# Graph layer in FP32 pieces: the first two column groups interleaved, the first half of adjacency rounded on VectorE, seven x tiles loaded later

## What is computed

```python
h   = maximum(layernorm(x), 0)          # mean and variance over the 256 features, eps 1e-5
agg = adj @ h
out = x + relu(agg @ W.T + b)
```

## Time and profile before

| what | us |
| --- | --- |
| median of 3 runs (380.69 to 380.96) | 380.95 |
| the profiled execution | 380.8 |
| span of its profile | 379.0 |
| TensorE busy in it | 375.1 |
| VectorE, ScalarE, GpSimd busy | 212.2, 181.8, 50.1 |

### The profile page before, as it was taken

How to read it: one execution, slowest core, us unless ns; L and a number is a source line. 1 busy time by engine, 2 the same in 40 slices (tenths; PEclk the granted TensorE clock), 3 DMA queues, 4 the chain that set the end, 5 groups by cost and what they waited for, 6 DMA issues and landing times.

```text
span 379.0 us, 4516 instructions
## 1 busy us (share of the span) xinstructions
PE 375.1 (99%) x1651; PEld 308.1 (81%) x1651; DVE 212.2 (56%) x294; ACT 181.8 (48%) x228; POOL 50.1 (13%) x88
## 2 busy tenths in 40 slices
PE   8999999999999999999999999999999999999997
PEld 4888888888888888888888888888888888888885
DVE  5999988874744453535564544444464444444424
ACT  5888776764443434343643343433355243434341
POOL 5687732320010000000001000000000100000000
PEclk9999999999999999999999999999999999999999
DMA  7989877577659565655566856565656775555203
GB/s 263 369 301 304 275 256 258 185 235 256 210 186 317 174 215 178 208 177 209 176 206 207 294 178 209 178 205 184 201 189 195 256 242 195 187 202 185 92 2 111
DMA packets 22774, 80.25 MB, mean 212 GB/s; under 512 B 2496, under 2 KB 2880, under 8 KB 22752
## 3 DMA queue, kind: packets, MB, share of 16 engines
q1 hardware_dynamic: 19584, 68.30, 54.1%
q0 software_dynamic: 3168, 11.67, 8.6%
HBM read 75.76 MB, written 4.19 MB: 211 GB/s over the span
## 4 chain that ended last, share of the span: by engine, by line
PE 98%; DMA 1%; DVE 0%; ACT 0%; POOL 0%; issue 0%; POOLq 0%
PE bank L421 92%; PE bank L463 6%; DMA x_sb<-x_dram 1%; ACT adj_hi L346 0%; POOL rstd L204 0%; ACT h_sb L352 0%; DVE out_sb L320 0%; DVE stats L240 0%; DVE mean_var L245 0%; DVE var_eps L249 0%; POOLq L200 0%
## 5 line engine op out<-in xcount | busy, mean ns | idle before, releaser
L421 PE MATMUL bank<-adj_hi,h_sb 128*128 128x512 f32 x1024 | 254.3, 389 | 0.2 <-ACT adj_hi L346 0.2
L229 DVE TENSOR_TENSOR adj_lo<-adj_in,adj_hi 128x1024 fp32r<-128x1024 f32 x126 | 154.6, 1227 | 145.7 <-ACT adj_hi L342 145.5
L421 PEld LDWEIGHTS bank<-adj_hi,h_sb 128*128 128x128 f32 x1024 | 192.0, 188 | 40.5 <-issue 0.5
L342 ACT ACTIVATE adj_hi<-adj_in 128x1024 fp32r<-128x1024 f32 x126 | 133.5, 1060 | 176.7 <-PE bank L421 174.5
L421 PE MATMUL bank<-adj_lo,h_sb 128*128 128x512 f32 x512 | 137.5, 389 | 0.0
L421 PEld LDWEIGHTS bank<-adj_lo,h_sb 128*128 128x128 f32 x512 | 96.1, 188 | 20.0
L204 POOL TENSOR_TENSOR rstd<-var_eps,minus_half 128x1 f32<-128x1 f32 x32 | 30.5, 954 | 3.4 <-DVE var_eps L249 0.8
L221 POOL DMA_DIRECT2D out_t_dram<-out_sb x3 | 2.2, 726 | 211.0 <-DVE out_sb L320 211.0
L352 ACT ACTIVATE h_sb<-centred,rstd 128x256 fp32r<-128x256 f32 x32 | 16.0, 499 | 3.6 <-POOL rstd L204 3.2
L362 ACT ACTIVATE centred<-x_sb,neg_mean 128x256 f32<-128x256 f32 x31 | 15.5, 500 | 2.1 <-DVE neg_mean L264 1.9
L270 DVE SCALAR_TENSOR_TENSOR h_sb<-centred,rstd,h_sb 128x256 fp32r<-128x256 f32 x32 | 15.3, 477 | 1.0 <-ACT h_sb L352 1.0
(11 more groups left out here) (25 smaller groups left out, 42.7 us busy)
## 6 DMA issues: line engine op xcount, KB each, us to landing
adj_in<-adj_t_dram SPq DMA_DIRECT2D x126, 512.0 KB, 3.6
xt_sb<-x_t_dram POOLq DMA_DIRECT2D x4, 1024.0 KB, 7.4
x_sb<-x_dram POOLq DMA_DIRECT2D x7, 512.0 KB, 6.5
out_t_dram<-out_sb POOLq DMA_DIRECT2D x3, 1024.0 KB, 4.9
adj_in<-adj_t_dram SPq DMA_DIRECT2D x4, 256.0 KB, 4.8
out_t_dram<-out_sb SPq DMA_DIRECT2D x3, 256.0 KB, 2.0
x_sb<-x_dram POOLq DMA_DIRECT2D x3, 128.0 KB, 4.6
w_sb<-w_t_dram POOLq DMA_DIRECT2D x1, 256.0 KB, 6.0
```

Source lines behind the costliest of these rows:

```text
L229: nc.vector.tensor_tensor(adj_lo[:, k, :], adj_in[:, k, :], adj_hi[:, k, :].bitcast(fp32), ALU.subtract).then_inc(s_lo, 1)
L342: nc.scalar.activation(adj_hi[:, k, :], adj_in[:, k, :], ACT.Copy).then_inc(s_hi, 1)
L421: last = nc.tensor.matmul(bank(g, kb, c)[:], h_sb[:, t, hp, kb * P:(kb + 1) * P], adj_parts[ap][:, n % U, chunk(c)], start=(t == 0 and (hp ...
```

## The change

- The order of units is now a list, `UNITS`. Groups 0 and 1 alternate tile by tile for tiles 0 to 23 (`LAG` = 8), then group 0 finishes with tiles 24 to 31, then group 1; groups 2 and 3 follow as before. The places of the split and of the output are counted from each group's end (`end_of`, `SPLIT`, `OUT`), so that for group 0 they are at units 60 and 64, for group 1 at 68 and 72. TensorE's wait for the products with w_lo moves to the first split.
- The halves that are loaded first are now both of tile 0: units 0 and 1 are groups 0 and 1 of it.
- `first_rounded`: VectorE makes `adj_hi` of the first half, between `centre_first` and `h_rest(0)`. ScalarE waits for that before it rounds the second half.
- SP issues x tile 1 after the third half of adjacency. GpSimd issues tiles 2 and 3 after `root(0)`, tiles 4 to 7 after `root(1)`.
- Both engines' lists around the first units are reordered: the layer norm of tile n - 1 is now finished beside unit n.
- The matmuls on constants become 9 of 512 columns and 1 of 256.

```diff
-    WARM_UP = 10
-    WARM_ON = 3
+    WARM_UP = 9
+    WARM_ON = 1
+    LAG = 8
+    UNITS = [(g, t) for t in range(TILES - LAG) for g in range(2)]
+    UNITS += [(g, t) for g in range(2) for t in range(TILES - LAG, TILES)]
+    UNITS += [(g, t) for g in range(2, GROUPS) for t in range(TILES)]
+        def end_of(g):
+            return max(n for n, u in enumerate(UNITS) if u[0] == g) + 1
+        SPLIT = {end_of(g) + SPLIT_AT: g for g in range(LAST)}
+        OUT = {end_of(g) + OUT_AT: g for g in range(LAST)}
...
             load_chunk(1, 0)
+            load_x(sp, 1)
             load_chunk(1, 1)
...
-            for i in range(1, U):
-                load_x(pool, i)
...
                 root(t)
                 if t == 0:
+                    load_x(pool, 2)
+                    load_x(pool, 3)
+                if t == 1:
                     load_x(pool, U)
...
+            def first_rounded():
+                dve.wait_ge(s_early[0][0], 16)
+                nc.vector.tensor_copy(adj_hi[:, 0, chunk(0)], adj_in[:, 0, chunk(0)]).then_inc(s_hi, 1)
...
             centre_first()
+            first_rounded()
             h_rest(0)
+            early_rest(0, 0)
+            early_rest(0, 1)
+            early_rest(1, 0)
             moments(1)
             minus_mean(1)
...
+            for n in range(EARLY, TILES + 1):
+                if n < TILES:
+                    moments(n)
+                    minus_mean(n)
+                adj_rest(n)
+                h_rest(n - 1)
...
             h_rounded(0)
-            early_rounded(0, 0)
+            act.wait_ge(s_hi, 1)
             early_rounded(0, 1)
+            early_rounded(1, 0)
+            early_rounded(1, 1)
             centre(1)
...
+            for n in range(EARLY, TILES + 1):
+                if n > EARLY:
+                    centre(n - 1)
+                adj_rounded(n)
+                h_rounded(n - 1)
...
+            def early_unit(n):
+                pe.wait_ge(s_hhi, 1)
+                pe.wait_ge(s_hi, made_chunk(n, 0))
+                add_up(n, [0], 0, 0)
+                pe.wait_ge(s_hlo, 1)
+                add_up(n, [0], 1, 0)
+                pe.wait_ge(s_hi, made_chunk(n, 1))
+                add_up(n, [1], 0, 0)
+                pe.wait_ge(s_lo, made_chunk(n, 0))
+                add_up(n, [0], 0, 1)
+                add_up(n, [1], 1, 0)
+                pe.wait_ge(s_lo, made_chunk(n, 1))
+                add_up(n, [1], 0, 1).then_inc(s_pe, 1)
```

More of the change, by code:

```diff
@@ L128, in x_piece, with made_chunk, made_unit @@
             return next(i for i, (a, b) in enumerate(X_PIECES) if a <= t < b)
-        def made_chunk(t, c):
-            return CHUNKS * t + c + 1
-        def made_tile(n):
+        def end_of(g):
+            return max(n for n, u in enumerate(UNITS) if u[0] == g) + 1
+        SPLIT = {end_of(g) + SPLIT_AT: g for g in range(LAST)}
+        OUT = {end_of(g) + OUT_AT: g for g in range(LAST)}
+        def made_chunk(n, c):
+            return CHUNKS * n + c + 1
+        def made_unit(n):
             return made_chunk(n, CHUNKS - 1) if n < EARLY else CHUNKS * EARLY + n - EARLY + 1
@@ L157, in _, with load_chunk @@
         def _(sp):
-            def load_chunk(t, c):
-                sp.dma_start(adj_in[:, t, chunk(c)], adj_v[:, t, chunk(c)]).then_inc(s_early[t][c], 16)
+            def load_chunk(n, c):
+                g, t = UNITS[n]
+                at = g * GW + c * BANK
+                sp.dma_start(adj_in[:, n, chunk(c)], adj_v[:, t, at:at + BANK]).then_inc(s_early[n][c], 16)
             def load_adj(n):
-                g, t = divmod(n, TILES)
+                g, t = UNITS[n]
                 if n >= U:
-                    sp.wait_ge(s_hi, made_tile(n - U))
-                    sp.wait_ge(s_lo, made_tile(n - U))
+                    sp.wait_ge(s_hi, made_unit(n - U))
+                    sp.wait_ge(s_lo, made_unit(n - U))
                 sp.dma_start(adj_in[:, n % U, :], adj_v[:, t, g * GW:(g + 1) * GW]).then_inc(s_adj[n % U], 16)
@@ L172, in _ @@
             load_chunk(1, 0)
+            load_x(sp, 1)
             load_chunk(1, 1)
-            for n in range(EARLY, GROUPS * TILES):
+            for n in range(EARLY, len(UNITS)):
                 load_adj(n)
@@ L227, in adj_rest, with early_rest @@
                 k = n % U
-                dve.wait_ge(s_hi, made_tile(n))
+                dve.wait_ge(s_hi, made_unit(n))
                 nc.vector.tensor_tensor(adj_lo[:, k, :], adj_in[:, k, :], adj_hi[:, k, :].bitcast(fp32),
                                         ALU.subtract).then_inc(s_lo, 1)
[L232 to L235, removed]
+            def first_rounded():
+                dve.wait_ge(s_early[0][0], 16)
+                nc.vector.tensor_copy(adj_hi[:, 0, chunk(0)], adj_in[:, 0, chunk(0)]).then_inc(s_hi, 1)
+            def early_rest(n, c):
+                dve.wait_ge(s_hi, made_chunk(n, c))
+                nc.vector.tensor_tensor(adj_lo[:, n, chunk(c)], adj_in[:, n, chunk(c)],
+                                        adj_hi[:, n, chunk(c)].bitcast(fp32), ALU.subtract).then_inc(s_lo, 1)
             def moments(t):
@@ L277, in _ @@
             centre_first()
+            first_rounded()
             h_rest(0)
+            early_rest(0, 0)
+            early_rest(0, 1)
+            early_rest(1, 0)
             moments(1)
             minus_mean(1)
[L281 to L286, removed]
-            early_rest(1, 1)
[L288 to L297, removed]
+            early_rest(1, 1)
+            for n in range(EARLY, TILES + 1):
[4 more added lines that the diff above has]
+                h_rest(n - 1)
             dve.wait_ge(s_b, 16)
@@ L322, in make_out @@
                                                    op0=ALU.max, op1=ALU.add).then_inc(s_sum, 1)
[L324 to L330, removed]
+            for n in range(TILES + 1, len(UNITS)):
+                if n in SPLIT:
+                    sums_rest(SPLIT[n])
+                if n in OUT:
+                    make_out(OUT[n])
+                adj_rest(n)
             sums_rest(LAST)
@@ L342, in adj_rounded, with early_rounded @@
                 nc.scalar.activation(adj_hi[:, k, :], adj_in[:, k, :], ACT.Copy).then_inc(s_hi, 1)
-            def early_rounded(t, c):
-                act.wait_ge(s_early[t][c], 16)
-                nc.scalar.activation(adj_hi[:, t, chunk(c)], adj_in[:, t, chunk(c)], ACT.Copy).then_inc(s_hi, 1)
+            def early_rounded(n, c):
+                act.wait_ge(s_early[n][c], 16)
+                nc.scalar.activation(adj_hi[:, n, chunk(c)], adj_in[:, n, chunk(c)], ACT.Copy).then_inc(s_hi, 1)
             def h_rounded(t):
@@ L385, in sums_rounded @@
                 if g < LAST:
-                    act.wait_ge(s_pe, (g + 1) * TILES)
+                    act.wait_ge(s_pe, end_of(g))
                 for i, (c, kb) in enumerate(GROUP_BANKS):
@@ L400, in _ @@
             act.wait_ge(s_b, 16)
[L401 to L407, removed]
+            for n in range(TILES + 1, len(UNITS)):
+                if n in SPLIT:
+                    sums_rounded(SPLIT[n])
+                if n in OUT:
+                    add_bias(OUT[n])
+                adj_rounded(n)
             add_bias(LAST)
@@ L415, in _, with add_up @@
             adj_parts = (adj_hi, adj_lo)
-            def add_up(g, t, chunks, hp, ap):
-                n = g * TILES + t
+            def add_up(n, chunks, hp, ap):
+                g, t = UNITS[n]
                 for kb in range(KB):
@@ L425, in add_up, with sum_unit @@
                 return last
[L427 to L442, removed]
+            def early_unit(n):
[11 more added lines that the diff above has]
+                add_up(n, [1], 0, 1).then_inc(s_pe, 1)
+            def sum_unit(n, chunks, arrived):
+                g, t = UNITS[n]
                 for hp, ap in PASSES:
@@ L446, in sum_tile @@
                             if g == 0:
-                                pe.wait_ge(s_hhi, n + 1)
-                            pe.wait_ge(s_hi, made_tile(n))
+                                pe.wait_ge(s_hhi, t + 1)
+                            pe.wait_ge(s_hi, made_unit(n))
                         elif ap == 1:
-                            pe.wait_ge(s_lo, made_tile(n))
+                            pe.wait_ge(s_lo, made_unit(n))
                         elif g == 0:
-                            pe.wait_ge(s_hlo, n + 1)
-                    last = add_up(g, t, chunks, hp, ap)
+                            pe.wait_ge(s_hlo, t + 1)
+                    last = add_up(n, chunks, hp, ap)
                 return last
@@ L482, in _ @@
             warm_up(WARM_ON, BANK // 2)
[L483 to L489, removed]
+            for n in range(EARLY):
+                early_unit(n)
+            for n in range(EARLY, len(UNITS) - U):
+                g, t = UNITS[n]
+                if g >= 2 and t == 0:
                     pe.wait_ge(s_sum, (g - 1) * SUMS)
[L492 to L495, removed]
+                if n in SPLIT:
```

(7 more changed lines are left out.)

## The result

| | before | changed |
| --- | --- | --- |
| median, ten runs each | 380.95 us | 381.84 us |
| lowest to highest | 380.58 to 381.27 | 381.05 to 382.4 |
| the profiled execution, and its span | 380.8, 379.0 | 381.05, 379.2 |

The ratio is 1.0021, 95% interval 1.0014 to 1.0029. The changed kernel is slower by 0.9 us, little more than the 0.76 that the prediction took as the least that can be told from no change, and its times spread twice as wide (1.35 us against 0.69). Its profile is of an execution at the low end of that spread and shows only 0.25 us of the loss; the traces of the experiments show the rest.

A forecast was written before the change was run, and what follows sets the result against it. TensorE's matmul pace was taken to bound everything behind 5.84 us, leaving only the start to win. An earlier first matmul gains 0.5, other parts cost nothing: 380.95 - 0.5 = 380.45 us, range 380.0 to 381.4.

The forecast's parts named there:

- the landing of x tile 2: VectorE's moments before unit 2: tile issued at about 4.5, landing 8.9 to 9.7, wanted at 8.81; hidden or 0.2 us stall.
- second rival: Late x tiles hold VectorE and so TensorE, up to 382.6 us; chance 0.10 within 0.76 of before, 0.06 slower.
- Tiles 4 to 7: Issued at about 9.3, landing 15.1 to 17.2, needed by 15.1 for unit 4; costs up to 2.1 us of TensorE's time.
- The load of the first half: First half of adjacency lands at 4.3 us, bounds 3.4 and 5.07, so first matmul at about 5.3.
- The first rival: The half lands no earlier, 4.8 to 5.1; first matmul at 5.6 to 5.9, time 380.7 to 381.0; chance 0.13.
- The copy: VectorE's rounding of the first half takes 0.66 us, bounds 0.41 and 0.69, hidden if the half lands by 4.41.
- Slack from an early start: Unit 2 starts 5.61 us behind the first matmul, at 10.91; adj_lo of unit 2 then has 0.6 to 0.7 slack.
- GpSimd's descriptors and VectorE: Skill's rule against the change: VectorE can lock GpSimd out of writing descriptors for the x tiles; no size given.
- third rival: Clock low at the first real matmuls, 0.42 instead of 0.2267 each, 0.8 to 2.4 us more; chance 0.08.
- ScalarE's rounding left the chain: Before the first matmul: rounding on VectorE takes ScalarE's 0.64 us off the chain, a gain of 0.63 at most.
- banks, splits, stores and the later groups: Interleaving and banks after the first units: slack shrinks from 70 us to some 9 and stays; cost nothing.

The follow-up runs named there:

- again: The changed kernel unchanged, run once more for a second trace; median 381.68 us.
- best_pool: Changed kernel with `rest_first`'s lists, moments of tile 1 and rounding of its h moved earlier, x loads of the kernel before; median 380.89 us.
- copy_alone: The kernel before with only VectorE's rounding of the first half (`first_rounded`) and ScalarE waiting for it; median 380.98 us.
- rest_first: Changed kernel; from unit 2 VectorE makes a unit's rest before the tile's moments, ScalarE rounds the unit before centring; median 380.8 us.
- loads_alone: The kernel before with only the changed x loads; order of units, rounding and constants as before; median 383.9 us.
- constants_back: The changed kernel with the constants' matmuls of before, 10 of 512 and 3 of 256 columns; median 381.87 us.

## Why the prediction was wrong

It said 380.45, within 380.0 to 381.4; it was 381.84.

- **The step that failed: the landing of x tile 2.** The second rival named the mechanism, VectorE held by a late x tile with the rest of a unit behind it, and priced tile 2 at 0.2 us of stall "at the worst". The price came from the earlier trace rows, tiles issued at 1.3 to 2.5, when SP had issued one to three halves of adjacency, 4.4 to 5.2 us. Issued at 4.5, when SP had issued 2 MB of it, tile 2 took 5.6, 6.5 and 7.5 us. The right row was there: the piece issued at 4.49 took 7.9, and I used it for tiles 4 to 7 only. With 6.5 to 7.5 for tile 2 (11.0 to 12.0, wanted at 8.8, slack 0.7) the same sum gives a stall of 1.5 to 2.5, and the forecast would have been slower. Measured: 1.1 and 1.2 us at unit 2, and none in the profiled execution, where tile 2 took only 5.6.
- **Tiles 4 to 7**: forecast 15.1 to 17.2 for a need at 15.1, measured 15.88 and a wait of 0.3 us. Right in mechanism and size. It was given the larger price of the two (up to 2.1 us, against 0.2) and was the smaller matter.
- **The load of the first half**: taken as 4.3, measured 5.21, and 4.26 to 5.28 over all traces. The bounds (3.4, 5.07) were nearly right. The value within them came from counting bytes, and the traces don't bear that out: without the x tiles the half landed no more reliably early. In the changed kernel the DMAs moved 42, 212 and 266 KB in the stretches of the earlier trace rows from 1 to 4 us, more than the 393 that were to be through at 3.9, and the half landed at 5.21 all the same. The first rival (5.6 to 5.9 for the first matmul) held in the profiled execution, and I gave it 0.13.
- **The copy**: 0.43 to 0.44 us, against 0.66 taken and 0.41 to 0.69 as bounds. The Trainium skill was right here ("VectorE: DVE Perf Modes", Mode 2×_2P: two results a cycle for a one-source float32 copy), and the 256-column form of the earlier trace rows, which took the same 0.41 for half the columns, misled me: it has pointer scalars and another operation.
- **Slack from an early start.** I carried unit 2's start over as "5.6 behind the first matmul". Where the start was early it was 5.74 (again), 5.88 (best_pool), 5.97 (copy_alone) and 6.30 (rest_first). The low clock took 0.24 of that in `copy_alone` and 0.46 in `rest_first`; the rest are waits for the second half or for h of tile 1, which ScalarE makes behind adjacency. Of the early start, 0.77, 0.34 and 0.49 us in `rest_first`, `copy_alone` and `best_pool`, unit 2 kept 0.08, nothing and 0.23; `again` kept most of it (0.62 of 0.75) up to the wait for tile 2. So even without late x tiles much of the gain would have been given back. This step was missing from the sum.
- **GpSimd's descriptors and VectorE.** The rule of the Trainium skill that I cited against the change ("DMA: Bandwidth & Descriptors", SWDGE vs HWDGE vs iDMA) was not the mechanism. The late tiles come in `loads_alone` as well, which has no copy and a VectorE without two-input work from 5.62 to 7.89, and they come sooner when SP's queue is short. No run here shows VectorE holding up a descriptor.
- **The clock**, third rival: not the cause of the loss, but not nothing. The granted clock is printed as full (1.00) for all these stretches, so its level is read from the matmuls' steps. The first two blocks below are TensorE's timeline, of the changed kernel and then of `rest_first`. In the first, nine constants' matmuls took 3.42 us, where the eight steps at 1.2 GHz alone take 3.4, so the clock was up well before their end. In the second the first real matmuls still ran low: three of them in 1.38, two steps in 0.99 where the changed kernel's first two took 0.53. That took 0.46 us of an early start of 0.77. The third block is `copy_alone` and the fourth the kernel before, with the same thirteen constants' matmuls: the first two real ones took 0.95 us in place of 0.70. So it isn't the shorter run of constants that costs here, but an early start that comes ahead of the rise. The Trainium skill says in the section cited in the prediction ("TensorE: Matmul & The Clock Gate", What's actually happening) that the moment of the rise differs from run to run. The traces agree: under the same constants' matmuls, begun at 0.78 each time, it lay between 3.3 and 3.6 in the changed kernel's first trace and behind 5.6 in `rest_first`. That is farther apart than the half microsecond either way that the section gives, and the traces decide.
- **Right**: ScalarE's rounding left the chain; banks, splits, stores and the later groups cost nothing; nothing behind unit 5 changed.

```profile
0.78 3.42 PE L496 MATMUL bank<-const-bfloat16-1.0 128*128 128x512 bf16 x9 [0.78 <-PEq L536]
```

```profile
0.78 4.21 PE L496 MATMUL bank<-const-bfloat16-1.0 128*128 128x512 bf16 x10 [0.78 <-PEq L536]
5.07 1.38 PE L440 MATMUL bank<-adj_hi,h_sb 128*128 128x512 f32 x3
```

```profile
5.50 0.95 PE L426 MATMUL bank<-adj_hi,h_sb 128*128 128x512 f32 x2
```

```profile
5.84 0.70 PE L421 MATMUL bank<-adj_hi,h_sb 128*128 128x512 f32 x2 [0.24 <-ACT adj_hi L346]
```


## What to carry to other kernels

A load that is issued later pays for the queue that it now stands behind: price it by a load that was issued at the same moment, not by its own earlier self. In an engine's strict list put what the bound engine waits for ahead of what may be late; here that alone gave back the loss. And where a kernel starts earlier, ask what feeds it by the second unit of work and at which clock TensorE would run by then: a start that data or clock can't follow is given back at once.

## What the runs showed of the hardware

- x tiles issued by GpSimd at 4.4 to 4.6 got no data until 8.0 to 8.7 where SP had issued six adjacency transfers before, and got it at 5.9 (issued at 4.35) when two of the six were held back.
- The very first large load landed 3.1 to 4.1 us after its issue over the 13 traces, and 3.1 to 4.0 in the five with the same loads around it (the changed kernel, `again`, `constants_back`, `loads_alone`, `rest_first`). This spread is larger than the gain the change was built on.
- The first step of TensorE behind a wait was 0.31 to 0.34 us instead of 0.2267, so each wait costs another 0.1 beyond its length.
